# A transformer block with 32 routed experts on one Trainium2 core: the expert blocks are taken in pairs, with a longer pipeline around each pair

## The reference

```python
shared_out = silu(x @ shared_gate_w.T) * (x @ shared_up_w.T) @ shared_down_w.T
routing_weights = softmax(x @ router_weight.T)            # 32 experts
_, top_idx = top_k(routing_weights + e_score_bias, 6)     # 6 of them per row
top_w = take_along_axis(routing_weights, top_idx) / their sum
gate, up = split(einsum('th,eih->tei', x, gate_up_proj))  # 128 each
hmid = silu(gate) * up
y = einsum('tei,ehi->teh', hmid, down_proj)
out = einsum('teh,te->th', y, combine) + shared_out
```

## Time and profile before

| | us |
|---|---|
| median of 3 runs | 917.71 (912.47 to 922.72) |
| profiled execution, own time | 926.67 |
| its span, first to last instruction | 924.9 |
| granted TensorE clock, mean of the span | 0.945 |
| granted clock, 394 to 654 us / 654 to 862 us | 0.93 / 1.00 |
| expert stage, first gate_up to last down projection | 394.3 to 861.6 |
| DMA, mean over the span | 170 GB/s |

### The profile page before, as it was taken

The page is one execution under the profiler, slowest core; times in us unless marked ns, Lnnn a source line. Parts: engine busy times, 40 slices in busy tenths (PEclk is TensorE's granted clock), DMA queues, the critical chain, the costliest instruction groups (busy, mean ns, idle before and its releaser), DMA issues.

```text
span 924.9 us, 14558 instructions
## 1 busy us (share of the span) xinstructions
PE 789.3 (85%) x4326; PEld 608.9 (66%) x4326; DVE 492.8 (53%) x1331; ACT 447.3 (48%) x1169; POOL 411.3 (44%) x420
## 2 busy tenths in 40 slices
PE   5998999989788775978788988889989888999993
PEld 4665576566476353567677867778878777888541
DVE  3585797887688333433333333243434434344897
ACT  5266656744442630055545454455666666666100
POOL 0000001667657666565555655554555555555200
PEclk9997999999989977989989999898999999999997
DMA  9200010232258935444555755454565555549796
GB/s 334 86 1 0 1 46 22 98 155 111 115 200 313 352 138 199 149 146 153 176 180 171 238 175 169 165 178 145 160 191 155 160 164 181 165 125 338 297 413 248
DMA packets 82461, 157.46 MB, mean 170 GB/s; under 512 B 14410, under 2 KB 55503, under 8 KB 82256
## 3 DMA queue, kind: packets, MB, share of 16 engines
q1 hardware_dynamic: 58192, 95.68, 31.9%
q0 software_dynamic: 19968, 56.67, 15.5%
q10 hardware_dynamic: 4224, 4.19, 1.3%
HBM read 87.10 MB, written 73.56 MB: 174 GB/s over the span
## 4 chain that ended last, share of the span: by engine, by line
PE 69%; DVE 9%; ACT 7%; another core or an unknown queue 6%; issue 5%; DMA 3%; SPq 1%; ACTq 0%; DVEq 0%
PE ps_wide L1302 22%; PE ps_wide L1308 13%; PE ps_narrow L1294 6%; PE ps_wide L1075 5%; PE ps_wide L950 3%; PE ps_kv L979 2%; DMA arena<-expert_outs 2%; PE ps_wide L1097 2%; PE ps_kv L1097 2%; PE ps_wide L1068 2%; PE ps_kv L1323 1%; PE ps_narrow L1088 1%; PE ps_kv L1383 1%; PE ps_narrow L1026 1%
## 5 line engine op out<-in xcount | busy, mean ns | idle before, releaser
L620 POOL DMA_INDIRECT expert_outs<-arena,dest x224 | 218.1, 974 | 202.2 <-DVE arena L1798 151.7
L512 POOL DMA_INDIRECT expert_rows<-arena,slot_i x192 | 193.0, 1005 | 250.4 <-DVE arena L1608 156.5
L1302 PE MATMUL ps_wide<-arena 128*128 128x128 f32 x1792 | 246.0, 282 | 7.1 <-issue 4.6
L1302 PEld LDWEIGHTS ps_wide<-arena 128*128 128x128 f32 x1792 | 226.0, 198 | 9.8 <-issue 6.1
L1788 DVE TENSOR_TENSOR arena<-arena,ps_wide 128x128 f32<-128x128 f32 x224 | 64.3, 287 | 268.5 <-ACT arena L863 203.5
L1308 PE MATMUL ps_wide<-arena 128*128 x448 | 147.5, 412 | 53.2 <-DVE arena L1788 35.1
L867 ACT COPY arena<-arena 128x512 f32 x224 | 138.5, 619 | 9.6 <-issue 4.1
L859 ACT COPY arena<-ps_narrow 128x256 f32<-128x256 f32 x224 | 83.0, 370 | 117.6 <-PE ps_narrow L1294 87.5
L1308 PEld LDWEIGHTS ps_wide<-arena 128*128 128x128 f32 x448 | 69.9, 196 | 68.2 <-issue 66.8
L1798 DVE TENSOR_SCALAR arena<-ps_wide,arena 128x256 f32<-128x256 f32 x224 | 107.6, 481 | 13.2 <-PE ps_wide L1308 7.5
L863 ACT ACTIVATE arena<-ps_wide 128x128 f32<-128x128 f32 x224 | 61.5, 274 | 91.2 <-PE ps_wide L1302 71.0
(11 more groups left out here) (232 smaller groups left out, 969.2 us busy)
## 6 DMA issues: line engine op xcount, KB each, us to landing
arena<-expert_rows SPq DMA_DIRECT2D x224, 160.0 KB, 2.2
arena<-expert_outs SPq DMA_DIRECT2D x48, 512.0 KB, 10.6
arena<-w_experts SPq DMA_DIRECT2D x32, 384.0 KB
expert_rows<-pad_row SPq DMA_DIRECT2D x33, 160.0 KB
out<-x ACTq DMA_DIRECT2D x8, 512.0 KB, 10.3
expert_outs<-arena,dest POOLq DMA_INDIRECT x224
x<-x SPq DMA_DIRECT2D x3, 1024.0 KB, 11.2
h_cols<-arena SPq DMA_DIRECT2D x6, 512.0 KB
```

Of the source, the lines that this page charges most:

```text
L512: nc.gpsimd.indirect_dma_start(rows, bass.IndirectOffsetOnAxis(ap=slots_i[b % 2][:, t, k:k + 1], axis=0), hrows[b % 2][:, t, :], None, bou ...
L620: nc.gpsimd.indirect_dma_start(outs, bass.IndirectOffsetOnAxis(ap=dest[:, u:u + 1], axis=0), yb[u], None, bounds_check=last_out, oob_is_er ...
L1302: last = mm(ps_wide[:, 0, u % 2, half * P:(half + 1) * P], wgu[:, u % 4, first:first + I], xbt[:, u % 2, c * P:(c + 1) * P], start=(c == 0 ...
```

## The change

Blocks are taken in pairs p (blocks 2p and 2p+1). What is done for both at once: the copy of the turned rows (128x512 instead of twice 128x256), the silu and the product (128x256 instead of twice 128x128), and their signals. The product is written over the silu (`hid`). The rows are turned two pairs ahead, and the down projection stands two pairs behind: PE does gate_up of pair p, turns pair p+2, projects pair p-2 down. Gate and up products go through three PSUM banks in turn (`gate_up_bank`), the third of which is one half of ps_kv; the shared units therefore use only the other half, and do their gate side, their up side and their down side apart, in pairs 1, 3 and 5 of a group of eight, instead of gate and up together.

Other parts: expert numbers are read eight at a time into registers (`experts_from`), as are the first rows on SP. ACT's silu of pair p waits for the down projection of pair p-2 (`s_y`) instead of a signal from gate_up. Routing weight and output row of an expert lie beside each other in the scattered row, and DVE copies both, two numbers per row, to a table `meta` two pairs ahead (`keep_meta`). SP may reload a row buffer once that copy is made (`s_meta`). Results wait in 14 buffers instead of 16. The number of matmuls, weight copies, DMAs and bytes stays.

The core of the diff:

```diff
+DUO = 2
+DUOS = BLOCKS // DUO
+DUOS_OF = UNROLL // DUO
+AT_ONCE = 8
+OUTS = UNROLL - 2
+METAS = UNROLL + BUF
 PART = TPH
 PARTS = NT // PART
...
+        def experts_from(engine, j):
+
+            return nc.values_load_multi_w_load_instructions(
+                table[0:1, 0, j:j + AT_ONCE], engines=(engine,), min_val=0, max_val=E - 1,
+                skip_runtime_bounds_check_because="the table's experts are kept under E when it is made")[1]
+
+        def unit_at(p):
+
+            n = p // DUOS_OF - FIRST_UNIT
+            return n if 0 <= n < len(UNITS) else None
+
+        def gate_up_bank(p):
+
+            return ps_kv[:, 1] if p % 3 == 2 else ps_wide[:, 0, p % 3]
...
             def load_blocks(g, first_round):
+                at_rows = nc.values_load_multi_w_load_instructions(
+                    table[0:1, 1, g * BUF:(g + 1) * BUF], engines=(SP,), min_val=0, max_val=E * REGION,
+                    skip_runtime_bounds_check_because="rows are kept within the padding block when the table is made")[1]
                 for u in range(BUF):
                     j = g * BUF + u
-                    at_row = first_row_of(j)
-                    if not first_round:
-
-                        sp.wait_ge(s_yc, j - BUF + 1)
+                    at_row = at_rows[u]
+                    if not first_round and u % DUO == 0:
+
+                        sp.wait_ge(s_meta, (j - BUF) // DUO + 1)
                     sp.dma_start(xb[:, u, :], rows[bass.ds(at_row, P), :]).then_inc(s_xb[u], 16)
...
-                nc.gpsimd.indirect_dma_start(outs, bass.IndirectOffsetOnAxis(ap=dest[:, u:u + 1], axis=0),
-                                             yb[u], None, bounds_check=last_out,
+                nc.gpsimd.indirect_dma_start(outs, bass.IndirectOffsetOnAxis(ap=meta_i[:, j % METAS, 1:2], axis=0),
+                                             yb[j % OUTS], None, bounds_check=last_out,
                                              oob_is_err=False).then_inc(s_put[u], 16)
...
-            def copy_block(j, u):
-                act.wait_ge(s_xbt, j + 1)
-                nc.scalar.copy(xbt[:, u % 2, :], ps_narrow[:, u % 2, 0:C * P]).then_inc(s_xbc, 1)
-
-            def silu(j, u):
-                act.wait_ge(s_gu, j + 1)
-                nc.scalar.activation(hsil[:, u % 2, :], ps_wide[:, 0, u % 2, 0:P], ACT.Silu).then_inc(s_hs, 1)
-
-            def copy_weights(j, u):
-                e = expert_of(ACTE, j)
-                return nc.scalar.copy(wgu[:, u % 4:u % 4 + 1, :], wall[:, bass.ds(e, 1), 0:DOWN])
+            def copy_rows_of(p):
+
+                act.wait_ge(s_xbt, p + 1)
+                nc.scalar.copy(xbt[:, p % 2, :], ps_narrow[:, p % 2]).then_inc(s_xbc, 1)
+
+            def silu(p):
+
+                if p < 2:
+                    act.wait_ge(s_gu, p + 1)
+                else:
+                    act.wait_ge(s_y, p - 1)
+                nc.scalar.activation(hid[:, p % 2, :], gate_up_bank(p)[:, 0:DUO * P], ACT.Silu).then_inc(s_hs, 1)
+
+            expert = {}
+
+            def copy_weights(p):
+
+                for j in range(p * DUO, (p + 1) * DUO):
+                    if j % AT_ONCE == 0:
+                        expert.update(zip(range(j, j + AT_ONCE), experts_from(ACTE, j)))
+                    last = nc.scalar.copy(wgu[:, j % 4:j % 4 + 1, :], wall[:, bass.ds(expert[j], 1), 0:DOWN])
+                return last
...
-            def steps(g, last, with_unit=False):
-                for u in range(UNROLL):
-                    j = g * UNROLL + u
-                    if not (last and u == UNROLL - 1):
-                        copy_block(j + 1, u + 1)
-                    if not (last and u >= UNROLL - 3):
-                        copy_weights(j + 3, u + 3)
-                    silu(j, u)
...
+            copy_weights(0).then_inc(s_wgu, 1)
+            copy_rows_of(0)
+            copy_weights(1)
+            copy_rows_of(1)
+            for p in range(DUOS):
+                if p + 2 < DUOS:
+                    act.wait_ge(s_xbt, p + 3)
+                    copy_weights(p + 2)
+                    copy_rows_of(p + 2)
+                silu(p)
+                if unit_at(p) is not None and p % DUOS_OF == 1:
+                    unit_silu(unit_at(p))
...
+            def turn_blocks(p):
+
+                for i in range(DUO):
+                    j = p * DUO + i
+                    u, ends = j % BUF, j >= BLOCKS - BUF
+                    if ends:
+                        pe.wait_ge(s_xb_end[u], 16)
+                    else:
+                        pe.wait_ge(s_xb[u], (j // BUF + 1) * 16)
+                    rows_in = xb_end if ends else xb
+                    for c in range(C):
+                        last = nc.tensor.transpose(ps_narrow[:, p % 2, (i * C + c) * P:(i * C + c + 1) * P],
+                                                   rows_in[:, u, c * P:(c + 1) * P], ident)
                 last.then_inc(s_xbt, 1)
 
-            def gate_up(j, u):
-                pe.wait_ge(s_xbc, j + 1)
-                for half in range(2):
+            def gate_up(p):
+
+                pe.wait_ge(s_xbc, p + 1)
+                bank = gate_up_bank(p)
+                for i in range(DUO):
+                    for half in range(2):
+                        for c in range(C):
+                            first = c * 2 * I + half * I
+                            last = mm(bank[:, (half * DUO + i) * P:(half * DUO + i + 1) * P],
+                                      wgu[:, (p * DUO + i) % 4, first:first + I],
+                                      xbt[:, p % 2, (i * C + c) * P:(i * C + c + 1) * P], start=(c == 0), stop=(c == C - 1))
+                if p < 2:
+                    last.then_inc(s_gu, 1)
+
+            expert = {}
+
+            def down(p):
+
+                pe.wait_ge(s_hm, p + 1)
+                for i in range(DUO):
+                    j = p * DUO + i
+                    if j % AT_ONCE == 0:
+                        expert.update(zip(range(j, j + AT_ONCE), experts_from(PE, j)))
+                    last = mm(ps_wide[:, 1, p % 2, i * D:(i + 1) * D], hid[:, p % 2, i * P:(i + 1) * P],
+                              wall[:, bass.ds(expert[j], 1), DOWN:DOWN + D], start=True, stop=True)
+                last.then_inc(s_y, 1)
+
+            def unit_side(w, n, done):
+
+                i, at = UNITS[n]
+                for m in range(C):
                     for c in range(C):
-                        first = c * 2 * I + half * I
-                        last = mm(ps_wide[:, 0, u % 2, half * P:(half + 1) * P], wgu[:, u % 4, first:first + I],
-                                  xbt[:, u % 2, c * P:(c + 1) * P], start=(c == 0), stop=(c == C - 1))
-                last.then_inc(s_gu, 1)
-
-            def down(j, e, u):
-                pe.wait_ge(s_hm, j + 1)
-                mm(ps_wide[:, 1, u % 2, 0:D], hmid[:, u % 2, :], wall[:, bass.ds(e, 1), DOWN:DOWN + D],
-                   start=True, stop=True).then_inc(s_y, 1)
-
-            def unit_gate_up(n):
+                        last = mm(ps_kv[:, 0, m * UNIT * P:(m + 1) * UNIT * P], w[:, c, m * P:(m + 1) * P],
+                                  shared_cols[i][c][:, at * UNIT * P:(at + 1) * UNIT * P], start=(c == 0), stop=(c == C - 1))
...
+            turn_blocks(1)
+            for p in range(DUOS):
+                if p == 2:
+                    pe.wait_ge(s_sx, BEFORE)
+                gate_up(p)
+                if p + 2 < DUOS:
+                    turn_blocks(p + 2)
+                if p >= 2:
+                    down(p - 2)
+                at, n = p % DUOS_OF, unit_at(p)
+                if n is not None and at == 1:
+                    unit_gate(n)
+                if n is not None and at == 3:
+                    unit_up(n)
+                if n is not None and at == 5:
+                    unit_down(n)
+                if at == DUOS_OF - 1 and p < 3 * DUOS_OF:
+                    (count, starts, find)[p // DUOS_OF](1, ps_kv[:, 0])
+            down(DUOS - 2)
+            down(DUOS - 1)
...
-            def middle(j, u):
-
-                dve.wait_ge(s_hs, j + 1)
-                v.tensor_tensor(hmid[:, u % 2, :], hsil[:, u % 2, :], ps_wide[:, 0, u % 2, P:2 * P], ALU.mult).then_inc(s_hm, 1)
-
-            def weigh(j, e, n, u, ends):
-
-                rows_in = xb_end if ends else xb
-
-                if not (isinstance(n, int) and n == 0):
-                    dve.wait_ge(s_put[u], n * 16)
-                v.tensor_copy(dest[:, u:u + 1], rows_in[:, u % BUF, bass.ds(e + D + E, 1)])
-                dve.wait_ge(s_y, j + 1)
-                v.tensor_scalar(yb[u], ps_wide[:, 1, u % 2, 0:D], rows_in[:, u % BUF, bass.ds(e + D, 1)], None,
-                                ALU.mult).then_inc(s_yc, 1)
+            def middle(p):
+
+                dve.wait_ge(s_hs, p + 1)
+                v.tensor_tensor(hid[:, p % 2, :], hid[:, p % 2, :], gate_up_bank(p)[:, DUO * P:2 * DUO * P],
+                                ALU.mult).then_inc(s_hm, 1)
+
```

(42 more changed lines are left out.)

185 lines of the change are left out of this document (52 added, 133 removed).

## The result

| | before | changed |
|---|---|---|
| median, us (range, runs) | 917.47 (912.47 to 922.72, 4) | 881.85 (880.07 to 891.63, 4) |
| profiled execution, own time / span | 926.67 / 924.9 | 880.65 / 878.8 |
| expert stage | 467.3 | 419.7 |
| its first / second half (112 blocks each) | 260.2 / 207.1 | 234.8 / 185.0 |
| first gate_up at | 394.3 | 391.1 |

The ratio is 0.9625 (0.9567 to 0.9683): faster, by 3.8%, against the forecast's 6.7%. Between the profiled executions it is 46.0 us: the stage 47.6 shorter, its start 3.2 earlier, the end 4.7 longer. (The chip of these runs has no number on record.

What follows compares the result with a forecast made beforehand. The prediction took PE's late signals to ACT as the bound. Matmuls 368 + 2, waits 10, restarts and clock 10, register loads 5, GpSimd and row loads 5: stage 400 instead of 467, forecast 856 us, range 828 to 904.

Steps and rivals of the forecast that it cites:

- What bounds the kernel: Expert stage: matmuls alone need 368 of 467.3 us; the other 99 are lost, mostly to PE's signals reaching ACT late.
- Depth: Rows turned two pairs ahead give ACT's copies 1.9 us to spare, the down projection over 3, against 0.71 before.
- waits longer than the spare time 10, restarts and the lower clock 10: Stage: 10 us for waits over 1.9 us (between 0 and 30), 10 for restarts and stretches at the lower clock.
- register loads, GpSimd and row loads: Stage: 5 us added for reading registers, 5 more for GpSimd's indirect DMAs and SP's reloads of row buffers.
- Register loads: PE, ACT and DVE read eight registers every fourth pair: 1.35 us taken for ACT, 5 us in all over 28 loads.
- rival 2: Eight registers read one by one on ACT, 2.4 us every fourth pair: 900 to 905 us, 880 likelier; chance 0.07.
- Signals' number: 446 signals vanish in the stage: counted as nothing, though the skill's 26 ns each would give up to 12 us.
- Start and end: Two more pairs turned first and two down projections last cost 2 us; the 63 us after the stage stay.
- Profiled against median: Profiled execution lies 9 us above the median; half taken as stage time, giving 856 us between 860 and 851.
- 1 (PE's own limit of 1.85 us a block): Second half's lost time is PE's own matmul supply; only the first half gains, 32 us: 886 to 890; chance 0.18.
- 3 (slower because lateness grows with the chain): Signals late by PE's queue; the change loses from 3.7 us lateness at every pair: 936 to 975 us; chance 0.06.
- 4, no change: Another bound sits just under the stage's 467 us, such as result scatter or row loads: 910 to 925; chance 0.06.

Runs made afterwards that it cites:

- chip 4: Kernel before and changed kernel, both unaltered, run again on another chip: 801.16 and 809.25 us, ratio 1.010.
- the first chip: The chip, without a number on record, of the first runs of the kernel before and the changed kernel: 917.47 and 881.85 us.
- single lateness: Kernel before, with ACT starting a one-number DMA and waiting for it after the turning signal at every fourth block: 898.50 us, ratio 1.119.

## Why the prediction was right in direction and too high in size

**What bounds the kernel.** Right, and the runs make it sharper: 368 us was the floor of the stage (372.3 reached on chip 4), the other 95 are what the first chip adds, 61.8 in the first half and 33.2 in the second (forecast: 48 + 18 and 34). The two traces differ in PE's late signals and what follows them; that these are all of the 95 is my reading. What the profile could not tell is that this lateness is not in the kernel alone: the same code takes 801 us on three other chips, and on the one of them on which it was traced itself (chip 4) its signals are on time. The forecast's direction thus hung on the chip: on chip 4 the same change would have made it wrong.

**Depth.** Right in kind. PE's idle time ahead of the down projection fell to 1.2 us (forecast: under 10). On the first chip the cost of lateness (stage above that of chip 4) fell from 95.0 to 44.8 us. The spare time of 1.9 measured 2.1.

**The term that was mis-sized** is "waits longer than the spare time 10, restarts and the lower clock 10". Together they are 44.8, of which 34.6 in the first half (234.8 − 200.2) and 10.3 in the second, which came out at 185.0, the upper end of the 173 to 185 named. The granted clock of the first half was 0.94, not above 0.96. Of the 44.8, 23 are lost in the six stretches in which PE gets its products in drips; the other 22 are close to the 20 of the forecast. The drips could not be read from the trace before, which has none. Depth could not hide them, since it is PE itself that gets nothing to do. The step that failed is that I took the late signals of the trace before over as they were, and counted what is longer than 1.9 us. In the changed kernel each came about twice as late (1.04 us for 0.46), and 29 of 112 turning signals were over 2 us late where 16 of 224 had been; the six ahead of the drips make 34 of their 116 us. Whether the longer queue does this, or the first chip was in another state in that run, is open. The waits also show less than all of the lateness, since a wait begins only when ACT is free: 147 us against 242 in the records of turning and gate_up.

The stage in sum, 419.7 for 400: 374.9 on chip 4 for the 370 of matmuls and depth (+4.9), 44.8 for 20 (+24.8), and nothing to be seen of the 10 for register loads, GpSimd and row loads (−10).

**Register loads.** Forecast 1.35 us for eight, bounds 0.30 and 2.4. Line 368 of the changed kernel on the first chip (ns min/median/max):

```profile
L368 ACTq TENSOR_LOAD <-table x28: 543/547/977, 381.6 to 794.0; - x28
...
L368 PEldq TENSOR_LOAD <-table x28: 587/604/967, 396.1 to 802.2; - x28
```

0.55 to 0.60 us. The 5 us for them were too many, and rival 2 falls. Nor had they cost anything before: the 17.0 us of "issue" ahead of the down projection, which I took for them, are waits for DVE's product whose signal has no record. Each of these down projections starts 0.15 us after the product's end, as those do that the profile puts down to DVE. The Trainium skill, "Runtime: NRT & Kernel Launch", section "Instruction fetch mechanics", has about 200 ns for each register even in bulk, which by estimate would be 1.6 us for eight. The trace, where the registers come from a table in SBUF, disagrees: about 40 ns for each one after the first (547 against 278).

**Signals' number.** Taken as nothing; by the Trainium skill, "TensorE: Matmul & The Clock Gate", section "The cost: per-tile semaphore tail", an estimate of up to 12 us was to be gained. On chip 4, where nothing covers it, the changed stage is 2.6 us longer, not 12 shorter: the row was right.

**Start and end.** "The 63 us after 861.6 stay" was wrong. GpSimd needs 1.28 us for a result block, and the last down projections follow each other faster than that, so it trails at the end. Its last scatter on the first chip, before and changed:

```profile
862.75 1.45 POOL L620 DMA_INDIRECT expert_outs<-arena,dest  x1 [0.30 <-issue]
```

```profile
816.58 0.97 POOL L638 DMA_INDIRECT expert_outs<-arena,meta  x1 [0.31 <-issue]
```

It ends 2.6 us behind the last down projection before (864.2 − 861.6), 6.7 now (817.55 − 810.8); the loads of the last stage come behind it. That is 4.1 of the 4.7. Stage and end together make the forecast's miss: stage 419.7 for 400, end + 4.7, start − 3.2.

**Profiled against median.** I gave the change half of the 9 us by which the profiled execution stood above the median. The profiled gain is 46.0, that of the medians 35.6, as if all of the 9 was in what the change removes (one profiled execution of each, so not shown). With that the forecast would have been 860.

**The range.** 881.85 lies just above the forecast's own range (830 to 881). It is inside the 828 to 904 because that was widened for rivals 1 and 2, whose mechanisms the runs refute: that part is luck.

**The rivals.** 1 (PE's own limit of 1.85 us a block): refuted, the second half of the changed kernel takes 1.65 us a block on the first chip (185.0 / 112), and the kernel before 1.55 on chip 4 (173.9 / 112). But the drips are a limit of PE's supply, in the changed kernel on the first chip and in the first half. 2: refuted above. 3 (slower because lateness grows with the chain): its time is refuted on the first chip, but not its premise. The mean lateness of turning went from 0.46 to 1.04 us, only not to 3.7 at every pair. On chip 4 the change is 1% slower by another way, which I had not among the rivals: nothing to hide, and something to pay (4, no change, had another bound behind it). The two traces show 0.9 us of it (stage + 2.6, end + 2.3, start − 4.0); the rest of the 8 us between medians lies between runs and was not located.

**Which depth.** On chips with signals on time, rows turned one pair ahead serve as well (805.1, stage 372.6), and the down projection must stay two behind (835.1, stage 401.8): PE's groups of the two runs, down one behind and turn one ahead, 365 to 766 us:

```profile
L1341 PE MATMUL ps_wide<-arena 128*128 x447 | 120.5, 392 | 15.9 <-issue 8.2 <-DVE arena L1824 5.9
```

```profile
L1343 PE MATMUL ps_wide<-arena 128*128 x448 | 115.2, 380 | 0.5 <-DVE arena L1826 0.5
```

With one pair in between PE waits at the projection. That this is because ACT copies for the pair two ahead before it takes the silu is my reading of the order, not shown by a run. How those two would do on a chip with late signals was not tried: none of the later runs met one.

**Open:** why PE's signals are late on the first chip, why the changed kernel's are later, and what the drips are. Theory A (held back while the sequencer issues) was never put to a test, since no later run met a late signal, and it can't be the whole: on chip 4 the sequencer issues in the same bursts and every signal that has a record takes 0.01 us. The first runs carry no number of their chip, so chip, its neighbours' work or its state are equally possible.

## What to carry to other kernels

A deeper pipeline is worth exactly the lateness that it covers beyond the spare time there was: work out both from a trace (0.7 and 2.1 us here), and take the lateness from the semaphores' records beside the waits. Hold each record against the start of the instruction that waits for it: up to a quarter of PE's and over a third of DVE's changes had none on the first chip, and each of those reads as a late signal or as "issue". Don't take the lateness over to the changed kernel as it is; here it doubled. Before tuning against a stall that no instruction explains, profile the same kernel on a second chip: here all of the gain, and 116 of 917 us, belonged to one. What is left on the three others is the price of the depth: more blocks in flight at the end, and an engine behind them that trails.

## What the runs showed of the hardware that was not expected

- The same kernel takes 917 us in the first runs and 801 on chips 13, 4 and 6. On chip 4 its granted clock is 0.968 against 0.945, and the part ahead of the expert blocks is 25 us shorter as well (368.9 against 394.3).
- A semaphore change by PE comes 0.01 us after the matmul's end on chip 4; on the first chip 0.5 to 0.6 us in the mean in the kernel before and 1.0 in the changed one, up to 7.0. Changes by ACT and DVE come after 0.01 us on the first chip too (kernel before).
- Records of semaphore changes can be missing from a trace: 4 of 672 of PE's on chip 4, 98 of 672 on the first chip, where 85 of 224 of DVE's product are missing as well.
- Eight registers read at once take 0.55 to 0.60 us, one takes 0.28 to 0.30.
- A DMA of one number, from issue on ACT to ACT's next work, takes 1.5 us at least and 2.0 to 2.2 in the mean.
- Idle PE time of about 3 us every eighth block brought the granted clock to 0.91 to 0.93; about 1.5 us every fourth block (1.01 + 0.47 in the event shown) left it at 1.00 (single lateness, 400 to 700 us).
